# Per-batch adapter slices by indexed transfers, and small adapter products in parts of the array

## What is computed

```python
c   = einsum('bct,bcd->bdt', x, cond_w[idx]) + fside[idx]      # 32x32 per batch
x1  = x + attention(c)                  # 16 heads of 16, causal, 32x32 per head and batch
def lora(v, W, A, Bm): return v @ W + (v @ A[idx]) @ Bm[idx]   # A[idx], Bm[idx]: rank 16
h   = silu(lora(x1, Wg, Ag, Bg)) * lora(x1, Wu, Au, Bu)        # 256 -> 1024
y2  = lora(h, Wd, Ad, Bd)                                      # 1024 -> 256
out = x1 + fwht(silu(y2 @ W1.T) * (y2 @ W3.T)) @ W2.T          # 256 -> 1024 -> 256
```

## Time and profile before

| | us |
|---|---|
| median of 3 runs (227.44 to 227.6) | 227.55 |
| the profiled execution, its own time | 229.15 |
| its span, first to last instruction | 227.4 |
| PE busy in it | 221.2 |
| POOL, ACT, DVE busy | 120.3, 100.2, 85.2 |

### The profile page before, as it was taken

How to read it: one execution, slowest core, us unless ns; L and a number is a source line. 1 busy time by engine, 2 the same in 40 slices (tenths; PEclk the granted TensorE clock), 3 DMA queues, 4 the chain that set the end, 5 groups by cost and what they waited for, 6 DMA issues and landing times.

```text
span 227.4 us, 3702 instructions
## 1 busy us (share of the span) xinstructions
PE 221.2 (97%) x1482; PEld 179.5 (79%) x1482; DVE 85.2 (37%) x142; ACT 100.2 (44%) x169; POOL 120.3 (53%) x93
## 2 busy tenths in 40 slices
PE   7799999999999999999999999999999999999995
PEld 2487787878788888888888888888888888888894
DVE  4986999988454342210042000202222222220211
ACT  2368799895953414750473000213445555440000
POOL 1028767637787216999999900180266666443000
PEclk9969999999999999999999999999999999999999
DMA  6965310004023100330011000031101100000211
GB/s 176 421 205 178 99 45 4 4 3 109 29 72 94 68 3 1 92 92 23 3 46 46 0 3 0 0 85 54 46 3 49 45 0 0 4 0 0 76 65 46
DMA packets 5345, 13.02 MB, mean 57 GB/s; under 512 B 720, under 2 KB 1360, under 8 KB 5072
## 3 DMA queue, kind: packets, MB, share of 16 engines
q1 hardware_dynamic: 4896, 11.72, 16.7%
q10 hardware_dynamic: 432, 1.07, 1.4%
HBM read 11.73 MB, written 1.05 MB: 56 GB/s over the span
## 4 chain that ended last, share of the span: by engine, by line
PE 84%; ACT 6%; DVE 5%; DMA 1%; issue 1%; POOL 1%; DVEq 0%; ACTq 0%
PE bank L387 27%; PE bank L389 26%; PE bank L391 26%; ACT k_x L679 4%; PE bank L406 1%; PE bank L489 1%; DMA index_i<-index 1%; DVE cond_sel L887 1%; DVE k_x L881 1%; ACT k_x L701 1%; DVE k_x L938 1%; PE bank L413 1%; ACT prob L695 1%; ACT v_tok L689 0%; POOL prob L1167 0%
## 5 line engine op out<-in xcount | busy, mean ns | idle before, releaser
L1180 POOL TENSOR_TENSOR h_lo<-tmp_b,h_hi 128x512 fp32r<-128x512 f32 x32 | 41.0, 1295 | 32.3 <-ACT h_hi L728 32.3
L387 PE MATMUL bank<-act_hi,w_hi 128*128 128x512 f32 x152 | 52.8, 392 | 0.1
L389 PE MATMUL bank<-act_lo,w_hi 128*128 128x512 f32 x152 | 52.4, 390 | 0.0
L391 PE MATMUL bank<-act_hi,w_lo 128*128 128x512 f32 x152 | 52.3, 389 | 0.0
L1026 DVE TENSOR_TENSOR tmp_b<-bank,tmp_a 128x512 f32<-128x512 f32 x32 | 21.1, 688 | 73.6 <-PE bank L391 41.1
L1142 POOL TENSOR_TENSOR w_lo<-raw,w_hi 128x512 fp32r<-128x512 f32 (+3 forms) x22 | 35.5, 1624 | 11.6 <-ACT w_hi L663 11.4
L387 PEld LDWEIGHTS bank<-act_hi,w_hi 128*128 128x128 f32 x152 | 28.5, 188 | 6.9 <-issue 1.1
L391 PEld LDWEIGHTS bank<-act_hi,w_lo 128*128 128x128 f32 x152 | 28.5, 188 | 6.0
L389 PEld LDWEIGHTS bank<-act_lo,w_hi 128*128 128x128 f32 x152 | 28.5, 188 | 5.8
L728 ACT ACTIVATE h_hi<-tmp_b 128x512 fp32r<-128x512 f32 x32 | 19.8, 632 | 27.0 <-DVE tmp_b L1026 27.0
L389 PE MATMUL bank<-h_lo,w_hi 128*128 128x512 f32 (+1 forms) x88 | 27.4, 370 | 0.0
(11 more groups left out here) (86 smaller groups left out, 256.2 us busy)
## 6 DMA issues: line engine op xcount, KB each, us to landing
raw<-w_stream SPq DMA_DIRECT2D x13, 256.0 KB, 2.7
raw<-w_stream SPq DMA_DIRECT2D x8, 384.0 KB, 3.3
raw<-w_stream SPq DMA_DIRECT2D x3, 512.0 KB, 3.5
k_x<-x_slots ACTq DMA_DIRECT2D x2, 512.0 KB, 6.5
tmp_b<-w_t SPq DMA_DIRECT2D x1, 1024.0 KB, 9.0
resid<-x_feat SPq DMA_DIRECT2D x1, 1024.0 KB, 10.7
out_feat<-tmp_b SPq DMA_DIRECT2D x3, 256.0 KB, 2.1
out_feat<-tmp_b SPq DMA_DIRECT2D x2, 128.0 KB, 1.8
```

The source lines that it names most:

```text
L387: pe.matmul(ps[:, :], w[0], x_hi, start=start, stop=False)
L389: pe.matmul(ps[:, :], w[0], x_lo, start=False, stop=False)
L391: last.append(pe.matmul(ps[:, :], w[1], x_hi, start=False, stop=stop))
L1180: pool.tensor_tensor(lo, tmp_b[:, n % 4, :], f32(hi), ALU.subtract).then_inc(prod_split, 1)
```

## The change

The adapter matrices are no longer part of the weight stream that ACT and POOL split (all weight batches now have 512 columns, in six places). Instead SP reads each batch's index from `index_i` into a register (`adapter`, a TENSOR_LOAD and register instructions) and issues a transfer whose address depends on it: `a_in` (16 per half, 64-byte pieces), `b_first` and `b_rest` (two transfers for each batch, 16 partitions), `b_down` (32), `a_down` (32, each 128 partitions x 8 pieces of 64 bytes). Indices are read anew in each of these groups. SP waits before `b_rest` until the last output projection of half 1 is full (`o`, 1, 1), and before `a_down` until `up` (1, 5) is full.

`adapters_in` now has 32 float32 matmuls of 128 rows by 32 columns of the array with 64 moving columns: each takes two batches. DVE keeps each batch's own block and spreads it (`own_slots`, two instructions), without a split. `gate_up_adapters` has eight float32 matmuls per pair of gate and up tiles, four in rows 0 to 63 for gate and four in rows 64 to 127 for up, all 128 columns of the array wide, with 128 moving columns. It is called for two pairs at once. The down adapters are one group of 256 matmuls of 32 array columns, which take the high and the low part of h apart, and 16 matmuls of 64 rows. The bias matmuls are one instead of two per tile, three warm-up matmuls are added before `conditioned(1, 0)`, half 0 and half 1 have six own column blocks instead of five (`ALONE`), and the lists of all engines and the bank table are rewritten.

```diff
-W_Q, W_K, W_V, W_OUT, W_A, W_GU = 0, 1, 2, 3, 4, 5
-W_D0 = W_GU + HC
-W_AD, W_D1, W_BD = W_D0 + 1, W_D0 + 2, W_D0 + 3
-W_F = W_BD + 1
...
+W_Q, W_K, W_V, W_OUT, W_GU = 0, 1, 2, 3, 4
+W_D = W_GU + HC
+W_F = W_D + 2 * DC
...
+COLS = DC * DC * P
+PLACES = 6
...
-ALONE = 5
+ALONE = 6
+KEEP_WARM = 3
...
+            def adapter(b):
+
+                return sp.value_load(index_i[0:1, NG + b:NG + b + 1], min_val=0, max_val=N - 1)
+
+            def load_a_in(s):
+                for b in range(BH):
+                    sp.dma_start(a_in[:, s, :, b, :].unsqueeze(2),
+                                 adapter_cols(P_A, 2 * DC)[:, :, bass.DynSlice(adapter(s * BH + b), 1), :])\
+                      .then_inc(a_in_loaded[s], 16)
+
+            def load_b(part, done, bs, m0, m1):
+
+                for b in bs:
+                    rows_ = bass.DynSlice(adapter(b) * R, R)
+                    blocks = w_stream[rows_, PACKED_AT[P_GU]:PACKED_AT[P_D0]].rearrange("r (m a k) -> r m a k", m=HC, a=2)
+                    for a in range(2):
+                        at = a * (P // 2) + b % SLOTS * R
+                        sp.dma_start(part[at:at + R, b // SLOTS], blocks[:, m0:m1, a, DC * P:]).then_inc(done, 16)
+
+            def load_b_first(s, part):
+
+                load_b(b_first, b_first_loaded[s], range(s * BH + part * BH // 2, s * BH + (part + 1) * BH // 2), 0, ALONE)
+
+            def load_b_rest(s):
+                load_b(b_rest, b_rest_loaded[s], range(s * BH, (s + 1) * BH), ALONE, HC)
+
+            def load_b_down():
+                for b in range(B):
+                    at = b // BH * (P // 2) + b % SLOTS * R
+                    sp.dma_start(b_down[at:at + R, b // SLOTS % GROUPS],
+                                 w_stream[bass.DynSlice(adapter(b) * R, R), PACKED_AT[P_BD]:PACKED_AT[P_F]])\
+                      .then_inc(b_down_loaded, 16)
+
+            def load_a_down():
+                for b in range(B):
+                    sp.dma_start(a_down[:, :, b, :].unsqueeze(2),
+                                 adapter_cols(P_AD, HC)[:, :, bass.DynSlice(adapter(b), 1), :]).then_inc(a_down_loaded, 16)
 
...
-            for n in range(STAGES, BATCHES):
-                load_weights(n)
+            sp.wait_ge(index_loaded, 16)
+            load_a_in(0)
+            load_weights(W_OUT)
+            load_weights(W_GU)
+            sp.wait_ge(had_made, 1)
+            sp.wait_ge(ident_made, 1)
+            sp.wait_ge(blk_made, HALVES)
+            sp.wait_ge(xc_hi_made, DC + 1)
+            load_b_first(0, 0)
+            load_weights(W_GU + 1)
+            load_b_first(0, 1)
+            load_weights(W_GU + 2)
+            load_weights(W_GU + 3)
+            load_a_in(1)
+            load_weights(W_GU + 4)
+            load_b_first(1, 0)
+            load_weights(W_GU + 5)
+            load_b_first(1, 1)
+            for m in range(6, HC):
+                load_weights(W_GU + m)
+            wait_full(sp, "o", 1, 1)
+            load_b_rest(0)
+            load_weights(W_D)
+            load_b_rest(1)
+            load_weights(W_D + 1)
+            load_b_down()
+            load_weights(W_D + 2)
+            load_weights(W_D + 3)
+            wait_full(sp, "up", 1, ALONE - 1)
+            load_a_down()
...
-                for fb in (fb_hi, fb_lo):
-                    last = pe.matmul(tile("xc", s, c)[:, :], ones[:, :], fb[:, s * BH:(s + 1) * BH, :], start=False,
-                                     stop=fb is fb_lo, skip_group_check=True)
-                full(last, "xc", s, c)
+                pe.wait_ge(fbias_made, s + 1)
+                full(pe.matmul(tile("xc", s, c)[:, :], ones[:, :], fbias[:, s * BH:(s + 1) * BH, :], start=False,
+                               stop=True, skip_group_check=True), "xc", s, c)
...
-            def adapters_in(s, c, *two):
-
-                w = weights(W_A)
-                pe.wait_ge(x1_split, DC * s + c + 1)
-                for a in two:
-                    ps = claim("z", s, a) if c == 0 else tile("z", s, a)
-                    last = both([ps], unit(w, a * DC + c), rows(act_hi, act_lo, c, [s]), c == 0, c == DC - 1)
-                    if c == DC - 1:
-                        full(last[0], "z", s, a)
+            def adapters_in(s):
+
+                ps = claim("z", s, 0)
+                pe.wait_ge(a_in_loaded[s], 16 * BH)
+                for c in range(DC):
+                    wait_read(pe, "o", s, c)
+                    for q in range(GROUPS):
+                        for a in range(2):
+                            for e in range(2):
+                                b = q * SLOTS + 2 * e
+                                at = s * HT + b * T
+                                last = pe.matmul(ps[64 * a + 32 * e:64 * a + 32 * e + 32, q * 2 * T:(q + 1) * 2 * T],
+                                                 a_in[:, s, a * DC + c, b:b + 2, :].rearrange("p b r -> p (b r)"),
+                                                 resid[:, c, at:at + 2 * T],
+                                                 start=(c == 0 and q == 0), stop=(c == DC - 1),
+                                                 skip_group_check=True)
+                full(last, "z", s, 0)
...
-            def gate_up_adapters(m, *ss):
-
-                w = weights(W_GU + m)
-                for a, name in enumerate(("gate", "up")):
-                    pe.wait_ge(z_split, 2 * ss[-1] + 2)
-                    last = both([tile(name, s, m) for s in ss], unit(w, a * (DC + 1) + DC),
-                                rows(aux_hi, aux_lo, a, ss), False, True)
-                    for s, ins in zip(ss, last):
-                        full(ins, name, s, m)
+                        both(tiles, unit(w, a * DC + c), rows(act_hi, act_lo, c, ss), c == 0, c == DC - 1)
+
+            def adapters_out(halves, weight, slots):
+
+                for q in range(GROUPS):
+                    for h, (name, s, m) in enumerate(halves):
+                        rows_ = slice(64 * h, 64 * h + 64)
+                        ins = pe.matmul(tile(name, s, m)[:, q * P:(q + 1) * P], weight(rows_, q),
...
+                                        slots[rows_, q].rearrange("p e n -> p (e n)"), start=False,
+                                        stop=True, skip_group_check=True)
+                        if q == GROUPS - 1:
+                            full(ins, name, s, m)
+
+            def gate_up_adapters(*pairs):
+
+                for s in sorted({s for s, _ in pairs}):
+                    pe.wait_ge(z_even, s + 1)
+                    wait_read(pe, "z", s, 0)
+                for s, m in pairs:
+                    if m < ALONE:
+                        pe.wait_ge(b_first_loaded[s], 2 * 16 * BH)
+                        part, k = b_first, m
+                    else:
+                        pe.wait_ge(b_rest_loaded[s], 2 * 16 * BH)
+                        part, k = b_rest, m - ALONE
+                    adapters_out([("gate", s, m), ("up", s, m)],
+                                 lambda rows_, q: part[rows_, s * GROUPS + q, k], z_slots[s])
...
+            def down(m):
+
+                tiles = [claim(f"d{m}", s, 0) for s in range(HALVES)]
                 for k in range(HC):
-                    pe.wait_ge(prod_split, SPLIT_COUNT["up", 1, k])
-                    last = both(tiles, unit(w, k), h_rows(k), k == 0, name == "zd" and k == HC - 1)
-                if name == "zd":
-                    for s in range(HALVES):
-                        full(last[s], name, s, 0)
-            w = weights(W_BD)
-            pe.wait_ge(prod_split, SPLIT_COUNT["zd", 1, 0])
-            for s in range(HALVES):
-                for m, name in enumerate(("d0", "d1")):
-                    last = both([down[name][s]], unit(w, m), rows(aux_hi, aux_lo, 0, [s]), False, True)
-                    full(last[0], name, s, 0)
+                    w = weights(W_D + 2 * m + k // 4)
+                    pe.wait_ge(prod_split, ORDINAL["up", 1, k] + 1)
+                    both(tiles, unit(w, k % 4), h_rows(k), k == 0, k == HC - 1)
+
+            def down_adapters_in():
+
+                ps = claim("zd", 0, 0)
+                pe.wait_ge(a_down_loaded, 16 * B)
+                for k in range(HC):
+                    for part in (h_hi, h_lo):
+                        for q in range(GROUPS):
+                            for s in range(HALVES):
+                                for e in range(2):
+                                    b = q * SLOTS + 2 * e
+                                    last = pe.matmul(ps[64 * s + 32 * e:64 * s + 32 * e + 32, q * 2 * T:(q + 1) * 2 * T],
+                                                     a_down[:, k, s * BH + b:s * BH + b + 2, :].rearrange("p b r -> p (b r)"),
+                                                     f32(part[s][:, k, b * T:(b + 2) * T]),
+                                                     start=(k == 0 and part is h_hi and q == 0),
```

(19 more changed lines are left out.)

508 lines of the change are left out of this document (255 added, 253 removed), and 21 rows, old and new, of the table EARLY_BANKS.

## The result

The changed kernel takes 338.54 us (median of 4 runs, 336.62 to 341.19), the kernel before 227.57 beside it: a ratio of 1.488, 95% interval 1.482 to 1.493. All ratios here use undisturbed runs only, so one may differ slightly from the quotient of the medians. My 224 us and my range to 246 were wrong. The profiled execution took 336.62 us with a span of 334.5.

A forecast was written before the change was run, and what follows sets the result against it. TensorE was taken to bound the kernel, with one new wait for `a_down` behind SP's list: `a_down` complete at 133.4 plus 90.5 of work behind it gives 223.9, forecast 224 us, range 213 to 246.

The forecast's parts named there:

- `b_rest` begins: SP may start `b_rest` at 68.2 us, once half 1's last output projection is full.
- `b_rest` to `a_down`: SP's 96 transfers at 0.37 us, 64 reads at 0.09 and three weight loads; `a_down` begins at 110.6 us.
- `a_down` to TensorE's first use of it: Packets of `a_down` take 20.8 us plus 2.0 to landing; complete at 133.4, TensorE waiting 7.1 us.
- from there to the end: TensorE work behind the wait: down adapters 9.0, `down(1)` 10.9, then 2.1 and 68.5, together 90.5 us.
- the price of a register read: On SP, each index read costs 0.09 us, range 0 to 0.33; slower than before above 0.145.
- SP's list ahead of `b_rest` has slack: SP's earlier transfers and reads were not priced; `b_rest` was taken to begin at 68.2 us.
- My sentence on what would make it wrong: Wrong too if `W_OUT` weights, now behind `a_in`, hold ACT ahead of the first exponentials; no size given.
- The added matmuls: On TensorE, new adapter matmuls and three warm-up matmuls add 31.2 us; parts in different rows overlap at full width.
- TensorE alone: Without waits for slices TensorE would end at 227.4 - 41.0 + 31.2 - 1.0 = 216.6 us.
- my "no wait" rival: TensorE never waits, reads near free and packets quick: 216.6 us, or 213.3; chance 0.56 jointly with the main forecast.
- The rewritten order of the attention: New engine order in attention counted at nothing; as a rival, it spends the gain there: about 227.4 us.
- The rival with dearer reads: Register reads on SP cost more, delaying `a_down` and ACT's down weights: 240.8 us at 0.33 a read; chance 0.28.

The follow-up runs named there:

- the bulk run: The changed kernel with seven plain transfers of the same bytes in place of the 224 small ones and 160 index reads: 223.26 us, ratio 0.982.
- the spread form: Against the bulk run, the 256 down-adapter matmuls split, 32 behind each chunk's six matmuls of the second down block: 221.84 us, ratio 0.974.
- The last kernel: Changed kernel with eight-index reads, long pieces, spread down adapters, reordered SP list, and ACT issuing half 1's `b_rest` where it waits: 221.60 us, ratio 0.9725.

## Why the prediction was wrong

The chain of terms was the right one, and it can be filled in with what the trace after shows:

| term | predicted | measured | difference |
|---|---|---|---|
| `b_rest` begins | 68.2 | 107.2 | +39.0 |
| `b_rest` to `a_down` (96 transfers, 64 reads) | 42.4 | 90.6 | +48.2 |
| `a_down` to TensorE's first use of it | 22.8 | 38.6 | +15.8 |
| from there to the end | 90.5 | 98.1 | +7.6 |
| sum | 223.9 | 334.5 | +110.6 |

**The step that failed is the price of a register read.** I bounded it "from above" at 0.33 us by the issue of one transfer, and chose 0.09 because a read moves one word. It costs 0.536 us with its check (the doubled reads): 0.268 for the load, 0.152 and 0.018 for the check, and about 0.1 that is in no row. No row of before had a load into a register or a check, so the upper bound had no ground; I should have left it open. Put into my own sum, 0.536 gives 68.2 + 35.5 + 34.3 + 1.1 + 29.0 + 2.0 + 90.5 = 260.6 us: this step accounts for 36.7 of the 110.6 us. The Trainium skill ("DMA: Bandwidth & Descriptors", Latency and other measured facts) gives about 600 ns for such a load; the trace does not bear it out as a floor, as the load alone has 268 ns. As a price of the whole read, 0.54 us with its check, it was close.

**A second step failed with it: that SP's list ahead of `b_rest` has slack.** I let `b_rest` begin as soon as the output projection of half 1 was full. But 96 transfers, 64 reads and 9 weight batches stand ahead of it from 6.36 us on, and they end at 106.5. I had priced only what stands behind the wait. With my own terms (6.4 + 105 x 0.37 + 64 x 0.33) that list would have ended at 66 us, and I would have called it free; at 0.54 and 0.50 it ends at 93. The rest up to the measured 106.5 holds the address instructions (about 0.08 us a transfer) and single long issues (up to 3.1 us in `a_in`). That is the 39.0 us of the table's first line. It also holds the weight batches, and ACT with them, so that attention waits (the 7.3 and 13.9 us) and the down projection (26.7). My sentence on what would make it wrong named this for `W_OUT` and only for the first exponentials.

**Sizes.** A back-to-back small transfer takes 0.50 us, not 0.37, and with real indices each also has its address instructions, some 0.08 us, which no term of my sum priced apart. A packet of 64 bytes takes 12.5 to 12.7 ns, within my 10 to 13.4; in the changed kernel this was hidden behind the reads. The down adapters took from 236.36 to 251.97, 15.6 us instead of 9.0: 16 groups at 0.45 are 7.2, less than my price; 5.6 are pauses, 1.6 come from the first four groups, which ran at the low clock after the wait of 21.3 us (0.85 us from start to start), and 1.2 stay open.

**What held.** The added matmuls: a call of the outer product for two pairs lasts from 63.42 to 65.41, 2.0 us against 2.1 from the earlier trace rows, so parts in different rows overlap at full width in float32; `adapters_in` goes from 97.66 to 98.69, 1.03 against 1.08. TensorE alone would end at 216.6 plus the 3.9 us of the dearer block (12.9 for 9.0) = 220.5; the bulk run had 220.6. Part of that is luck, since errors cancel. Its first matmul of q, k and v starts at 12.61 us against 16.29 before, 3.7 us earlier, where I had counted 0.3 (the 1.0 from the clock less 0.7 for the warm-up matmuls; the bias matmuls that I put at nothing are in it too, and 0.7 us of it are those of half 1, which now stand behind). Yet SP sees the output projection of half 1 full only 0.9 us ahead of my 68.2, at 67.31, so most of that gain was lost again up to there, 1.2 us of it in the pause at the scores. So my "no wait" rival gave nearly the right time for a kernel that was not there. The rewritten order of the attention makes TensorE wait for no other engine by more than about 1 us as long as the slices are early; what it costs otherwise is open.

The rival with dearer reads had 0.28, and its mechanism is what happened. Its time, 240.8 at the upper bound, was too low by the same two faults.

## What to carry to other kernels

Before you price what a new kind of instruction costs TensorE, write out the whole list of the engine that issues it, from its first instruction on, at a pessimistic price: a list that never pauses moves every later transfer, also those that have nothing to do with the change. Do not price a register read by the rows of weight loads or DVE instructions: here it cost 0.536 us against their 0.09 and 0.18. Read many indices at once, ahead of where they are needed. And if a change removes TensorE work but the time rises, replace its transfers by a few plain ones: that one run says whether the idea or its delivery is at fault.

## What the runs showed that I had not expected

- Of the 0.536 us of a read, 0.255 go with its bounds check. The load of eight words takes 0.525 us, twice as long as that of one.
- One small transfer between two reads holds SP for 0.320 us; the same transfer back to back holds it for 0.420, with single ones up to 1.3 us (the rows of the `b_down` line, after and with fixed addresses).
- 64-column matmuls in a block of 256 pause 0.6 to 2.0 us after each 128 records in the changed kernel, with nothing in the trace that they wait for (with seven plain transfers first after 253, then after 128); among 512-column matmuls they don't. A pause can also cost the clock: 0.55 was granted behind the second pause of the bulk run.
- Weights that are read with a stride are loaded more slowly: the median load of the down adapters is 150 to 152 ns with a stride of 8 words, and 110 ns without, and a round of the spread form takes 2.78 us instead of 2.61. The last kernel pays this 1.4 us for its long pieces.
